# Second expert weight and gated tile to TensorE unsplit, as plain fp32, with the weight read in place

## The reference

```
x = x + 0.5 * ffn(_layernorm(x), ...)
x = x + attn(_layernorm(x), ...)          # RWKV: time mixing and channel mixing
x = x + 0.5 * ffn(_layernorm(x), ...)     # the same weights as the first
```

```
for e in range(E):
    h = jax.nn.silu(xt @ w1[e]) * (xt @ w3[e])
    out = out + w[:, e:e + 1] * (h @ w2[e])
```

## Time and profile before

| | before |
|---|---|
| median of three runs | 1434.15 us |
| the runs | 1430.66 to 1434.25 us |
| span of the profiled execution | 1435.0 us |
| TensorE matmul busy | 1202.8 us (84%) |
| VectorE, ScalarE, GpSimd busy | 997.3, 815.8, 764.9 us |
| first and last addition of rows, layer 0 | 522.63 and 648.38 us |
| first and last addition of rows, layer 1 | 1299.46 and 1425.39 us |

### The profile page before, as it was taken

The page is one execution under the profiler, slowest core; times in us unless marked ns, Lnnn a source line. Parts: engine busy times, 40 slices in busy tenths (PEclk is TensorE's granted clock), DMA queues, the critical chain, the costliest instruction groups (busy, mean ns, idle before and its releaser), DMA issues.

```text
span 1435.0 us, 22901 instructions
## 1 busy us (share of the span) xinstructions
PE 1202.8 (84%) x7016; PEld 1004.3 (70%) x7016; DVE 997.3 (69%) x1941; ACT 815.8 (57%) x1550; POOL 764.9 (53%) x521
## 2 busy tenths in 40 slices
PE   4799999999998278982387599999999999618985
PEld 3688888888886257771277488888888888517774
DVE  5487677677787557876757647767677688628874
ACT  5366566566555167761453646656666566328873
POOL 3275575574600469992412347466385360058996
PEclk9599999999999589995789679999999999759998
DMA  9100100100001922325100500010010000552223
GB/s 282 37 1 1 37 0 0 37 0 0 1 1 33 341 41 41 47 41 157 37 0 1 151 1 1 1 37 0 0 37 0 0 1 1 184 205 40 44 44 63
DMA packets 60133, 69.87 MB, mean 49 GB/s; under 512 B 6048, under 2 KB 49312, under 8 KB 59936
## 3 DMA queue, kind: packets, MB, share of 16 engines
q1 hardware_dynamic: 51920, 58.94, 13.0%
q0 software_dynamic: 8160, 10.26, 4.6%
HBM read 49.58 MB, written 20.66 MB: 49 GB/s over the span
## 4 chain that ended last, share of the span: by engine, by line
PE 65%; DVE 11%; DMA 9%; issue 5%; ACT 4%; POOL 4%; POOLq 1%; DVEq 1%; ACTq 0%; SPq 0%
PE ps L1366 19%; PE ps L1368 17%; PE ps L1367 17%; PE ps L1433 8%; DMA sum_dram<-ys,slot_token 7%; POOL xs_dram L648 2%; PE ps L1423 1%; POOL probs L671 1%; DVE hidT L1160 1%; DVE parts L1143 1%; PE ps L1497 1%; PE ps L1345 1%; DVE mixT L1307 1%; DVE tokT L1009 1%; DMA xs<-xs_dram 1%
## 5 line engine op out<-in xcount | busy, mean ns | idle before, releaser
L742 ACT ACTIVATE probs<-ps,negmax 128x128 f32<-128x128 f32 (+7 forms) x256 | 189.8, 742 | 121.3 <-DVE negmax L1054 119.7
L1054 DVE TENSOR_REDUCE negmax<-ps 128x1 f32<-128x128 f32 (+7 forms) x256 | 191.5, 751 | 74.9 <-PE ps L1423 72.8
L748 ACT ACTIVATE probsT<-ps 128x512 fp32r<-128x512 f32 x288 | 167.9, 597 | 102.2 <-PE ps L1433 100.6
L1059 DVE TENSOR_TENSOR probsT<-ps,probsT 128x512 fp32r<-128x512 f32 x288 | 194.7, 686 | 44.1 <-ACT probsT L748 43.4
L595 POOL TENSOR_TENSOR crossed<-crossed,rope 128x512 f32<-128x512 f32 x68 | 89.0, 1310 | 180.7 <-ACT crossed L725 180.7
L1433 PE MATMUL ps<-square,probs 128*128 128x128 f32 x1152 | 169.2, 274 | 0.0
L1366 PE MATMUL ps<-keysT,queriesT 128*128 128x512 f32 (+3 forms) x384 | 143.2, 373 | 20.7 <-DVE queriesT L1043 18.9
L627 POOL TENSOR_TENSOR parts<-experts,parts 128x1024 fp32r<-128x1024 f32 x46 | 134.0, 2914 | 26.7 <-ACT parts L797 26.7
L1433 PEld LDWEIGHTS ps<-square,probs 128*128 128x128 f32 x1152 | 134.0, 141 | 19.0
L1075 DVE SCALAR_TENSOR_TENSOR h<-ps,rowinv,h 128x256 f32<-128x256 f32 x256 | 123.0, 480 | 19.5 <-PE ps L1368 14.1
L1368 PE MATMUL ps<-keysT,queriesT 128*128 128x512 f32 (+3 forms) x384 | 135.1, 352 | 0.0
(11 more groups left out here) (228 smaller groups left out, 3421.3 us busy)
## 6 DMA issues: line engine op xcount, KB each, us to landing
experts<-in_L_ffn_w_dram SPq DMA_DIRECT2D x42, 512.0 KB
xs_dram<-blank SPq DMA_DIRECT2D x2, 2967.0 KB, 17.6
xs<-xs_dram SPq DMA_DIRECT2D x46, 129.0 KB, 2.0
w_in<-in_L_ffn_wq_dram SPq DMA_DIRECT2D x8, 512.0 KB, 4.0
wo_in<-in_L_ffn_wo_dram SPq DMA_DIRECT2D x8, 512.0 KB, 5.2
probs<-in_L_attn_x_dram SPq DMA_DIRECT2D x2, 1024.0 KB, 5.8
sum_dram<-h SPq DMA_DIRECT2D x2, 1024.0 KB
w_in<-in_L_ffn_wk_dram SPq DMA_DIRECT2D x8, 128.0 KB, 4.0
```

What stands on the lines that cost most here:

```text
L742: act.activation(probs[:, i % 2, k, 0:w], ps[:, 2 * slot_n:2 * slot_n + 2, :].rearrange("p b n -> p (b n)")[:, 0:w], ACT.Exp, bias=negmax[ ...
L748: act.activation(probsT[:, m % 3, 0, :], ps[:, 4 + m % 2, :], ACT.Copy).then_inc(S["probsT_high"], 1)
L1054: dve.tensor_reduce(negmax[:, m:m + 1], ps[:, s:s + 2, :].rearrange("p b n -> p (b n)")[:, 0:w], AX.X, ALU.max, negate=True).then_inc(S["m ...
L1059: dve.tensor_tensor(probsT[:, m % 3, 1, :], ps[:, 4 + m % 2, :], probsT[:, m % 3, 0, :].bitcast(F32), ALU.subtract).then_inc(S["probsT_low ...
```

## The change

The second weight is no longer split: `parts2`, ScalarE's and GpSimd's `split_w2` and their semaphores go. hidT has one part, copied by ScalarE as plain fp32; VectorE's `take_hid` goes. `down` becomes four fp32 matmuls instead of twelve in fp32r, and they read the weight where it lies in `experts`, at an address from the expert's number, which TensorE now loads itself. `take_ys` on VectorE gets a wait for its own engine's `take_meta` of the same tile, which used to be implied.

```diff
--- before.py
+++ after.py
@@ -261,7 +261,7 @@
             ys = sb("ys", [P, 2, D], c=phase)
             xsT = sb("xsT", [P, 2, 2, DC, P], F32R, c=phase)
             hid = sb("hid", [P, 2, F], c=phase)
-            hidT = sb("hidT", [P, 2, 2, F], F32R, c=phase)
+            hidT = sb("hidT", [P, 2, F], c=phase)
         with ExitStack() as phase:
             sb("x_place_too", [P, NT, D], c=phase)
             kT_low0 = sb("kT_low0", [P, IC // 2, HALF], F32R, c=phase)
@@ -335,7 +335,6 @@
 
             with ExitStack() as tiles_phase:
                 parts13 = sb("parts13", [P, 2, 2, 2 * DC * F], F32R, c=tiles_phase)
-                parts2 = sb("parts2", [P, 2, 2, FC * D], F32R, c=tiles_phase)
 
             xT = sb("xT", [P, DC, 1 + T], c=phase)
             kT_low1 = sb("kT_low1", [P, IC // 2, HALF], F32R, c=phase)
@@ -380,8 +379,8 @@
             "turn_done probsT_high probsT_low pv_done attnT_high attnT_low squared out_ps out_added xT_clear "
             "logits_ps routing_ps routed pick_ready scattered gap_ready gap_exp "
             "rstd_ready rows_copied base_ready base_out meta_ready gate_open added sum_in_first sum_in_last "
-            "xs_turned xsT_high xsT_ready up_done silu_done hid_ready hid_turned hidT_high hidT_ready down_done ys_ready "
-            "w13_high w13_low w2_high w2_low "
+            "xs_turned xsT_high xsT_ready up_done silu_done hid_ready hid_turned hidT_ready down_done ys_ready "
+            "w13_high w13_low "
             "mix_ready v_done decay_done decay_used vw_ready u_done r_done r_ready r_used ck_done ck_relu ck_sq "
             "rows_in shift_ready gained scaled biased kT_high kT_ready ck_split ck_split_low xT_high xT_low "
             "cv_done cv_sig cv_used x_final"
@@ -620,13 +619,6 @@
                     group(f, g, ORDERS[True])
                 group(f, KVH - 1, ORDERS[False])
 
-            def split_w2(f, tau, par):
-
-                e = pool.value_load(owner[0:1, bass.ds(tau, 1)], min_val=0, max_val=E - 1)
-                pool.wait_ge(S["w2_high"], NS * f + tau + 1)
-                pool.tensor_tensor(parts2[:, par, 1], experts[:, bass.ds(e, 1), 2 * DC * F:], parts2[:, par, 0].bitcast(F32),
-                                   ALU.subtract).then_inc(S["w2_low"], 1)
-
             def add_rows(f, tau, par):
 
                 pool.wait_ge(S["ys_ready"], NS * f + tau + 1)
@@ -649,18 +641,13 @@
                             out=xs_dram, out_offset=bass.IndirectOffsetOnAxis(ap=slot[:, k, t:t + 1], axis=0),
                             in_=rows_out[:, k, t, :], in_offset=None).then_inc(S["scattered"], 16)
                 pool.wait_ge(S["owner_ready"], f + 1)
-                split_w2(f, 0, 0)
                 pool.wait_ge(S["base_out"], 16 * (f + 1))
                 if f == 0:
                     pool.wait_ge(S["pad_out"], 16)
-                split_w2(f, 1, 1)
                 add_rows(f, 0, 0)
-                split_w2(f, 2, 0)
                 add_rows(f, 1, 1)
                 with pool.Fori(1, (NS - 1) // 2) as k:
-                    split_w2(f, 2 * k + 1, 1)
                     add_rows(f, 2 * k, 0)
-                    split_w2(f, 2 * k + 2, 0)
                     add_rows(f, 2 * k + 1, 1)
                 add_rows(f, NS - 1, 0)
 
@@ -790,12 +777,6 @@
                     act.activation(parts13[:, par, 0, block], experts[:, bass.ds(e, 1), block], ACT.Copy
                                    ).then_inc(S["w13_high"], 1)
 
-            def split_w2(f, tau, par):
-                e = expert(tau)
-                if not isinstance(tau, int) or tau >= 2:
-                    act.wait_ge(S["down_done"], NS * f + tau - 1)
-                act.activation(parts2[:, par, 0], experts[:, bass.ds(e, 1), 2 * DC * F:], ACT.Copy).then_inc(S["w2_high"], 1)
-
             def take_xs(f, tau, par):
 
                 act.wait_ge(S["xs_turned"], NS * f + tau + 1)
@@ -810,7 +791,7 @@
 
             def take_hid(f, tau, par):
                 act.wait_ge(S["hid_turned"], NS * f + tau + 1)
-                act.activation(hidT[:, par, 0], ps[:, 6, :], ACT.Copy).then_inc(S["hidT_high"], 1)
+                act.activation(hidT[:, par], ps[:, 6, :], ACT.Copy).then_inc(S["hidT_ready"], 1)
 
             def moe(f):
                 sqrt()
@@ -837,8 +817,6 @@
                     if after > 1:
                         split_up(f, tau + 2, par)
                     take_hid(f, tau, par)
-                    if after > 0:
-                        split_w2(f, tau + 1, 1 - par)
 
                 step(0, 0)
                 step(1, 1)
@@ -1155,14 +1133,10 @@
                 dve.wait_ge(S["silu_done"], NS * f + tau + 1)
                 dve.tensor_tensor(hid[:, par, :], gated[:, par, :], ps[:, 2 * par + 1, :], ALU.mult).then_inc(S["hid_ready"], 1)
 
-            def take_hid(f, tau, par):
-                dve.wait_ge(S["hidT_high"], NS * f + tau + 1)
-                dve.tensor_tensor(hidT[:, par, 1], ps[:, 6, :], hidT[:, par, 0].bitcast(F32), ALU.subtract
-                                  ).then_inc(S["hidT_ready"], 1)
-
             def take_ys(f, tau, par):
 
                 dve.wait_ge(S["down_done"], NS * f + tau + 1)
+                dve.wait_ge(S["meta_ready"], NS * f + tau + 1)
                 dve.tensor_scalar(ys[:, par, :], ps[:, 7, 0:D], slot_weight[:, par:par + 1], None, ALU.mult
                                   ).then_inc(S["ys_ready"], 1)
 
@@ -1210,7 +1184,6 @@
                     take_meta(f, tau, par)
                     if after > 1:
                         split_up(f, tau + 2, par, e)
-                    take_hid(f, tau, par)
 
                 step(0, 0)
                 step(1, 1)
@@ -1481,13 +1454,14 @@
                 last.then_inc(S["hid_turned"], 1)
 
             def down(f, tau, par):
+                e = pe.value_load(owner[0:1, bass.ds(tau, 1)], min_val=0, max_val=E - 1)
                 pe.wait_ge(S["hidT_ready"], NS * f + tau + 1)
-                pe.wait_ge(S["w2_low"], NS * f + tau + 1)
                 if not (isinstance(tau, int) and NS * f + tau == 0):
                     pe.wait_ge(S["ys_ready"], NS * f + tau)
                 for c in range(FC):
-                    last = products(ps[:, 7, 0:D], [hidT[:, par, part, c * P:(c + 1) * P] for part in range(2)],
-                                    [parts2[:, par, part, c * D:(c + 1) * D] for part in range(2)], c == 0, c == FC - 1)
+                    place = slice(2 * DC * F + c * D, 2 * DC * F + (c + 1) * D)
+                    last = pe.matmul(ps[:, 7, 0:D], hidT[:, par, c * P:(c + 1) * P], experts[:, bass.ds(e, 1), place],
+                                     start=(c == 0), stop=(c == FC - 1))
                 last.then_inc(S["down_done"], 1)
 
             def moe(f):
```

## The result

| | before | after |
|---|---|---|
| median of four runs | 1434.2 us | 1444.88 us (1442.73 to 1446.98) |
| ratio | | 1.0076, interval 1.0056 to 1.0097 |
| span of the profiled execution | 1435.0 us | 1443.6 us (its own time 1445.4) |
| additions 0 to 22, layer 0 | 125.75 us | 129.42 us |
| additions 0 to 22, layer 1 | 125.93 us | 129.73 us |

The change makes the kernel 0.76% slower. Of the 8.6 us between the two spans 7.5 lie in the expert loops. Another 1.2 lie between them, where no instruction was changed. That stretch (addition 22 of layer 0 to addition 0 of layer 1) was 651.1 us before, 652.3 after, and 647.6 to 651.3 in the twelve experiments, which do not touch it either; it moves by more than 1.2 us by itself.

What follows compares the result with a forecast made beforehand. Bound: the chain of waits between row additions two tiles apart, not GpSimd. A pair: 11.53 + 0.07 + 0.33 = 11.93, say 11.9 us; the layers' 1.9 + 2.1 = 4.0 us on 1434.15 gave 1438 us, range 1427 to 1448.

Steps and rivals of the forecast that it cites:

- forecast A: Main forecast for the expert loop: additions 5.1 and 6.8 us apart, 1438 us (own range 1433 to 1442), chance 0.47.
- B: Slower rival: every gatekeeper comes after VectorE's split, all addition intervals 6.15 to 6.2 us, 1446 us; chance 0.22.
- C: Faster rival: TensorE's register load is hidden, a pair of tiles takes 11.48 us, 1429.5 us; chance 0.25.
- (1): GpSimd's split of the second weight goes: only the third kind of addition interval disappears, a gain of 3.6 us in all.
- (2): ScalarE's copy of the second weight goes, 46 of 1.06 us: nothing, between 0 and a gain of 0.5.
- (3): VectorE's low part of hidT leaves the chain: down products could start 0.3 us after the turn, 0.38 earlier.
- (4): TensorE's expert-number load stands exposed behind the turn of xs: 0.75 us to first product; with (3), +0.07 us per pair.
- The 0.68 that this was set against: Time in us from turn of xs to first down product in the kernel before, against 0.75 forecast.
- The page's figure: A floor of about 600 ns for the register load, not taken; it would make both layers some 6 us longer.
- (5): Four plain fp32 down products replace twelve: 2.05 us from first product to ys against 1.72, +0.33 per pair.
- (6): The added wait in take_ys is for a cast that ended a tile earlier: 0, at most 0.05.
- margin: Time by which ys is ready before the landing at the additions between: 0.8 us before, about 0.3 forecast after.

Runs made afterwards that it cites:

- e5: The kernel before without GpSimd's split of the second weight, the twelve products kept: 1432.64 us, ratio 0.9985.
- e3: The changed kernel with ScalarE copying the second weight as plain fp32 to a fixed address and no expert-number load on TensorE: 1425.05 us, ratio 0.9929.
- e1: The changed kernel with TensorE's load of the expert's number moved ahead of the turn of xs: 1426.63 us, ratio 0.9933.
- e4: The changed kernel with VectorE's split of the first weight waiting until the due addition's gatekeeper has run: 1438.0 us, ratio 1.0016 to the kernel before.
- e12: The kernel before with xs freed early by two one-column VectorE copies as its only edit: 1435.63 us, ratio 1.0005.
- e8: The changed kernel with the expert number loaded early, VectorE's split behind the gatekeeper and xs freed early: 1410.34 us, ratio 0.9829.

## Why the prediction was right, and where not

The direction was its larger chance (0.42 slower), the time lies in the range of 1427 to 1448, and the mechanism is that of forecast A: additions at 5.3 and 6.8 us, every second gatekeeper at 1.07. But 1444.88 is outside A's own 1433 to 1442 and beside B's 1446, and B did not happen: the gatekeepers between stay at 0.18. More than half of the chance for slower, 0.22, stood on B, and A's 1438 was closer to no change than to the result, so the direction was in part luck. The range held the right mechanism with one term too small, and it was wide because it spanned C to B.

- *(1) The split's going* was put at -3.6 us. e5: 2 us in the medians, 3.2 in the trace. Right in the trace, somewhat high by the medians; that it would be no more, though GpSimd was busiest, is right as well.
- *(2) ScalarE's copy*: nothing. e3 keeps such a copy and is as fast as e1. Right.
- *(3) hidT's low part*: without cover the products were to start 0.3 us behind the turn. e1: 0.27. Right.
- *(4) The register load* is the step that failed, as a size. It stands exposed behind the wait, as I read from the loop's register operation, but it makes 0.97 us from turn to product, not 0.75. Up to the end of the load and its own register operations the sum was good: 591.0 less 590.37 is 0.6 us. Behind them I had about 0.1 for the address operation and the gaps, and it is 0.3. The upper bound (ScalarE's longest load, +0.27 for both terms) rested on the load alone, and the load was no longer than its model: 302 ns on TensorE, 278 on ScalarE.
- *The 0.68 that this was set against* came from one pair and was low as well: over such pairs the mean is 0.76 in layer 0 and 0.84 in layer 1. So (3) and (4) together cost 0.22 and 0.11 us a pair, where the sum had 0.07. The rest of what is missing lies in the way from addition to turn (0.01 and 0.13 longer, forecast 0), in the pair before (11.56 and 11.54, taken as 11.53) and in rounding 11.93 to 11.9, which took 0.3 us from each layer's 107.4. Together the pair is 12.1 where 11.9 was forecast, and 18 pairs make the 3.5 us by which the loops came out longer (7.5 against 4.0).
- *The page's figure.* The Trainium skill (DMA: Bandwidth & Descriptors, Latency and other measured facts) has about 600 ns for such a load. The rows here say 302, and the measurement decides. The estimate by the page, some 6 us more than my sum and so 1444, lies nearer to the time, but by luck: what it has too much in the load stands in for the operations and gaps around it.
- *(5) Plain fp32*: 2.05 from first product to ys forecast, 2.03 measured, 1.98 in e1. Right.
- *(6) The added wait* stands in front of ys. Nothing is seen of it: the 2.03 us to ys hold it, and were forecast without it.
- *Rival C* (the load hidden) was priced at 1429.5. e1 makes its condition true and gives 1426.6, with a pair of 11.33 where C had 11.48. *Rival B*'s margin was forecast at 0.3 us and is 0.3: in the changed kernel the ys of the tile between ends at 587.57, and the slot copy that waits for the landing starts at 587.87.
- The reading of the chain was incomplete. It held the landing and the pair, but not the loop through ys, the load of xs and the turn (5.86 us, e4), nor what (3) implies and e12 shows, that easing the path over xs gains nothing while VectorE's hidT stands. Neither decides the change's own time; both decide what can be gained after it.

## What to carry to other kernels

Where an engine takes over a load of a register from memory, place it ahead of the engine's last wait, not behind: here the same load cost 0.70 us of the path behind a wait (0.97 against 0.27) and nothing in front of it (0.27 in e1, 0.28 in e3, which has no load), and that decided between 0.7% faster and 0.8% slower. The busiest engine of a loop need not be its bound; follow one period of the chain, and then ask for the next loop just below it, since several of nearly equal length hide each other's gains. Price an operation with all that its sequencer does up to the first instruction that uses it.

## What the hardware showed unexpectedly

- VectorE and GpSimd held each other up in both directions here. A gatekeeper of 0.19 us took 1.07 when VectorE's split had begun first. A VectorE copy of 128x2 from SBUF to SBUF took up to 2.59 us (median 2.38) beside GpSimd's split, 0.16 without it; a 128x1 copy took 0.15 beside the same split. Why the second column matters no run here shows.
- The indirect DMA on GpSimd depends on which engine was first. In e8 (530 to 625 us) it takes 1.55 to 1.56 us where it starts 0.01 to 0.09 us ahead of VectorE's split, and 2.45 to 2.61 where the split started 0.05 to 0.21 us ahead of it.
- Between a short gatekeeper and its DMA lie 0.43 to 0.47 us in e4, behind a wait for ys, in all tiles of layer 0 but one (0.15), and 0.15 to 0.16 in e1 and e5 behind a wait of 2.2 to 2.4 us for a landing; in the changed kernel and in e8 a landing gives 0.16 to 0.45. A pause alone doesn't tell which, and no run here shows what does.
- One fp32 matmul of 128x256 shows as two records 0.216 us apart from a fixed address (eight records 1.89 us in e3). From a register address the eight take 1.94 us in e1 and 1.99 in the changed kernel.
